# Reordered steps in the attention half and an earlier first gather, in a fused attention and mixture-of-experts kernel

## The reference

```python
xn = layernorm(x)                           # x: 8 x 512 tokens, 256 channels, float32
out = x + attention(xn) + experts(xn)

# attention: 16 heads of 16 features, causal
A = tril(1 + s + s*s/2)                     # s = q.k/4, a Taylor series in place of exp
y = (A @ v) / (row sums of A);  attention = y @ Wo.T

# experts: 8, the best 2 for each token, their weights a softmax over the two logits
y_e = (silu(xn @ W1[e]) * (xn @ W2[e])) @ W3[e]     # 256 -> 512 -> 256
```

## Time and profile before

| | |
|---|---|
| time, median of 3 runs | 669.97 us (669.42 to 671.02) |
| profiled execution | 669.97 us, span 668.2 us |
| TensorE busy | 96% of the span |
| VectorE, ScalarE, GpSimd busy | 61%, 51%, 51% |
| mean granted TensorE clock | 0.984 |

### The profile page before, as it was taken

The page is one execution under the profiler, slowest core; times in us unless marked ns, Lnnn a source line. Parts: engine busy times, 40 slices in busy tenths (PEclk is TensorE's granted clock), DMA queues, the critical chain, the costliest instruction groups (busy, mean ns, idle before and its releaser), DMA issues.

```text
span 668.2 us, 16297 instructions
## 1 busy us (share of the span) xinstructions
PE 640.6 (96%) x5351; PEld 493.3 (74%) x5351; DVE 409.9 (61%) x1067; ACT 341.9 (51%) x515; POOL 344.1 (51%) x381
## 2 busy tenths in 40 slices
PE   8799999999999999888999999999999999999994
PEld 6465666666666666546888888888888888888883
DVE  6776878787878585785984445444444544444452
ACT  3577878787877686764653223232322323232231
POOL 3255555546463736463464555555555545455542
PEclk9799999999999999987999999999999999999998
DMA  4643555455434435447533333334342333333332
GB/s 133 143 121 105 123 158 129 151 128 162 81 109 107 124 89 159 113 143 274 179 59 59 51 65 50 61 55 66 51 66 50 57 58 52 64 52 64 52 49 24
DMA packets 37773, 64.05 MB, mean 96 GB/s; under 512 B 8288, under 2 KB 25824, under 8 KB 37696
## 3 DMA queue, kind: packets, MB, share of 16 engines
q0 software_dynamic: 16704, 28.12, 21.4%
q1 hardware_dynamic: 20432, 34.24, 20.1%
q10 hardware_dynamic: 560, 0.66, 0.3%
HBM read 27.72 MB, written 22.68 MB: 75 GB/s over the span
## 4 chain that ended last, share of the span: by engine, by line
PE 87%; DVE 6%; ACT 2%; DMA 2%; issue 2%; ACTq 0%; POOL 0%; POOLq 0%; DVEq 0%
PE banks L1173 30%; PE banks L1194 15%; PE banks L1053 10%; PE banks L1035 8%; PE banks L1073 7%; PE banks L1182 5%; PE banks L1082 4%; PE banks L1117 4%; PE banks L1162 2%; PE banks L1102 1%; ACT T L530 1%; PE banks L1108 1%; DVE xTl L737 1%; PE banks L1091 1%; DMA out<-yo,xw 1%
## 5 line engine op out<-in xcount | busy, mean ns | idle before, releaser
L493 POOL DMA_INDIRECT out<-yo,xw x71 | 112.2, 1581 | 155.7 <-DVE yo L993 102.3
L622 ACT ACTIVATE sTh<-banks 128x512 fp32r<-128x512 f32 x71 | 42.5, 598 | 192.3 <-PE banks L1182 192.3
L473 POOL TENSOR_SCALAR_AFFINE_SELECT T<-T 128x512 f32<-128x512 f32 x128 | 80.6, 641 | 109.9 <-ACT T L536 41.7
L985 DVE TENSOR_TENSOR sTl<-banks,sTh 128x512 fp32r<-128x512 f32 x71 | 49.0, 691 | 118.0 <-ACT sTh L622 118.0
L1173 PE MATMUL banks<-w12h,xgh 128*128 x284 | 118.5, 417 | 0.9 <-DVE xgl L976 0.9
L1173 PE MATMUL banks<-w12l,xgh 128*128 x284 | 112.8, 397 | 0.0
L1173 PE MATMUL banks<-w12h,xgl 128*128 x284 | 112.6, 396 | 0.0
L482 POOL DMA_INDIRECT xg<-xs_scr,glist x71 | 73.4, 1033 | 21.5 <-issue 19.0
L1053 PE MATMUL banks<-T,vau 128*17 128x512 f32 (+3 forms) x1024 | 77.2, 441 | 0.2 <-POOL T L473 0.2
L1035 PE MATMUL banks<-Q,K 32*128 32x256 f32 (+2 forms) x1024 | 71.2, 363 | 6.0 <-DMA K<-Kt 2.8
L464 POOL DMA_INDIRECT xs_scr<-xb,slots x64 | 63.5, 993 | 18.8 <-issue 10.0
(11 more groups left out here) (172 smaller groups left out, 1212.6 us busy)
## 6 DMA issues: line engine op xcount, KB each, us to landing
Q<-Q SPq DMA_DIRECT2D x128, 64.0 KB, 2.3
w12r<-w SPq DMA_DIRECT2D x16, 512.0 KB, 4.8
out<-xa SPq DMA_DIRECT2D x16, 256.0 KB, 2.5
w3r<-w SPq DMA_DIRECT2D x8, 512.0 KB, 7.1
K<-Kt SPq DMA_DIRECT2D x124, 32.0 KB
xa<-x SPq DMA_DIRECT2D x7, 512.0 KB, 4.7
xg<-xs_scr,glist POOLq DMA_INDIRECT x71, 2.9
out<-yo,xw POOLq DMA_INDIRECT x71, 3.8
```

The source lines that it names most:

```text
L473: e.affine_select(out=v, in_=v, pattern=[[0, 4], [1, P]], compare_op=ALU.is_ge, fill=-1.0, base=0, channel_multiplier=-1).then_inc(s["g_mk ...
L493: e.indirect_dma_start(out, bass.IndirectOffsetOnAxis(xw[:, t % 4, NE:NE + 1].bitcast(U32), 0), yo[:, t % 2, :], None, compute_op=ALU.add) ...
L985: e.tensor_tensor(sTl[:], banks[:, 5, :], sTh[:].bitcast(F32), ALU.subtract).then_inc(s["v_st"], 1)
```

## The change

- The next batch's first K half is made first (quarter 1) and its Q half second (quarter 2), at the start too; `move_k` comes before `move_q` for it.
- VectorE takes the steps of `slot_b` as TensorE does: in quarters 0 and 2 step c comes before `normalise`.
- `place_rows` runs before `slot_b` in quarter 1 (so before `xTl`), `rsqrt` a little earlier, `w12_low` of quarter 2 after `slot_b`.
- Each send of batches 0 to 6 comes one slot earlier.
- In batch 7 the list work comes later relative to `o` and `normalise`; step G goes to `slot_c` of the last quarter.
- GpSimd issues the first gather between the second and third mask of the last quarter, after waits for the list and the sent rows.
- SyncE's w3 loads start in part one quarter earlier and are spread over later waits.
- TensorE's wait for all misc banks stands before the loop, so before `up(1, 0)`.

```diff
@@ slot_b, slot_c, sends_after
     elif qd == 2:
-        steps = [("c", b + 1, 1)]
+        steps = [("c", b + 1, 0)]
-    return steps + ([("t", ...)] if n else []) + ([("G", 0, 0)] if n == NQ - 1 else [])
+    return steps + ([("t", ...)] if n else [])
     if b == LAST:
-        return [("y", b, 0)] if qd == 3 else []
+        return [("G", 0, 0), ("y", b, 0)] if qd == 3 else []
-    return ([("c", b + 1, 0)] if qd == 1 else []) + [("v", ...), ("v", ...)]
+    return ([("c", b + 1, 1)] if qd == 1 else []) + [("v", ...), ("v", ...)]
-    k = 3 * qd + min(m, 2)
-    if k == 0:
-        return (b - 1, 7, 8) if b else None
-    i = k - (3 if b == LAST else 5)
+    i = 3 * qd + min(m, 2) - (3 if b == LAST else 4)
-FIRST = (("x", 0, 0), ("x", 0, 1), ("c", 0, 0), ("c", 0, 1), ...)
+FIRST = (("x", 0, 0), ("x", 0, 1), ("c", 0, 1), ("c", 0, 0), ...)
@@ sync_program
                     for h in range(2):
+                        move_k(e, b + 1, 0, h)
+                    for h in range(2):
                         move_q(e, b + 1, 0, h)
-                    for h in range(2):
-                        move_k(e, b + 1, 0, h)
@@
+            e.wait_ge(s["p_av"], NQ - 1)
             e.wait_ge(s["d_g1"], 16)
+            load_w3(0)
+            load_w3(1)
+            load_w12(13)
             e.wait_ge(s["p_av"], NQ)
-            for n in range(4):
-                load_w3(n)
-            load_w12(13)
-            e.wait_ge(s["p_t"], NQ)
-            for n in range(4, 6):
-                load_w3(n)
+            load_w3(2)
             store_out(LAST, 0)
             store_out(LAST, 1)
+            load_w3(3)
+            e.wait_ge(s["a_th"], 2)
+            load_w3(4)
+            e.wait_ge(s["p_t"], NQ)
+            load_w3(5)
+            e.wait_ge(s["a_th"], 3)
             done(e, "G", 0, 0)
             e.wait_ge(s["v_te"], 1)
-            for n in range(6, 8):
-                load_w3(n)
+            load_w3(6)
             e.wait_ge(s["p_o"], 2 * NBATCH)
             load_w12(14)
+            e.wait_ge(s["a_th"], 4)
+            load_w3(7)
@@ gpsimd_program, in mask(n)
                     if sends_after(n, m):
                         send(*sends_after(n, m))
+                    if n == NQ - 1 and m == 1:
+                        done(e, "G", 0, 0)
+                        e.wait_ge(s["d_xs0"], 512)
+                        e.wait_ge(s["d_xs1"], 512)
+                        e.wait_ge(s["d_z"], 32)
+                        e.wait_ge(s["p_s"], 6 * NQ - 8)
+                        gather(0)
@@ vector_program, before_b
-                elif n == NQ - 3:
+                elif n == NQ - 2:
+                    tile_gaps()
+                elif n == NQ - 1:
+                    all_rows()
+                elif qd == 1 and b < LAST:
+                    places(b)
+                    place_rows(b)
+                elif qd == 2 and b < NBATCH - 2:
+                    variance(b + 2)
+                elif qd == 3 and b < LAST:
+                    top(b + 1, 1)
@@ after_b (n == NQ - 3: tiles, NQ - 2: tile_rows(0), NQ - 1: expert_ends)
-                elif qd == 1 and b < LAST:
-                    place_rows(b)
-                if n == NQ - 2:
-                    w12_low(8)
+                if qd == 2 and (b, qd) in W12_LOW_WITH:
+                    w12_low(W12_LOW_WITH[b, qd])
@@ after_c (n == NQ - 3: tile_starts, NQ - 2: tile_rows(1), NQ - 1: experts)
                 elif qd == 2 and b < LAST:
                     top(b + 1, 0)
+                    if b < NBATCH - 2:
+                        rsqrt(b + 2)
@@ the loop of vector_program
-                items = slot_b(n)
-                if n % 4 in (0, 2) and n // 4 < LAST:
-                    items = [i for i in items if i[0] != "c"] + [i for i in items if i[0] == "c"]
-                for item in items:
+                for item in slot_b(n):
                     step(*item)
@@ tensor_program
+            for m in range(3):
+                e.wait_ge(s[f"m{m}"], USED[m])
             for t in range(1, NT + 1):
                 if t < NT:
                     expert_of(t)
                     up(t, 0)
-                if t == 1:
-                    for m in range(3):
-                        e.wait_ge(s[f"m{m}"], USED[m])
                 transpose_s(t - 1)
```

More of the change, by code:

```diff
@@ L27 @@
 W12_WITH = {(1, 1): 0, (1, 2): 1, (2, 1): 2, (2, 2): 3, (3, 1): 4, (3, 2): 5, (4, 1): 6, (4, 2): 7, (7, 0): 8}
-W12_LOW_WITH = {(1, 2): 0, (1, 3): 1, (2, 2): 2, (2, 3): 3, (3, 2): 4, (3, 3): 5, (4, 2): 6, (4, 3): 7}
+W12_LOW_WITH = {(1, 2): 0, (1, 3): 1, (2, 2): 2, (2, 3): 3, (3, 2): 4, (3, 3): 5, (4, 2): 6, (4, 3): 7, (7, 2): 8}
 F32 = mybir.dt.float32
@@ L56, in slot_b @@
     elif qd == 2:
-        steps = [("c", b + 1, 1)]
+        steps = [("c", b + 1, 0)]
     else:
         steps = [("o", b - 1, 0)] if b else []
-    return steps + ([("t", (n - 1) // 4, (n - 1) % 4)] if n else []) + ([("G", 0, 0)] if n == NQ - 1 else [])
+    return steps + ([("t", (n - 1) // 4, (n - 1) % 4)] if n else [])
 def slot_c(n):
@@ L68, in slot_c @@
     if b == LAST:
-        return [("y", b, 0)] if qd == 3 else []
+        return [("G", 0, 0), ("y", b, 0)] if qd == 3 else []
     if qd == 3:
         return ([("o", b - 1, 1)] if b else []) + [("y", b, 0), ("C", b + 1, 0)]
-    return ([("c", b + 1, 0)] if qd == 1 else []) + [("v", b + 1, 2 * qd - 2), ("v", b + 1, 2 * qd - 1)]
+    return ([("c", b + 1, 1)] if qd == 1 else []) + [("v", b + 1, 2 * qd - 2), ("v", b + 1, 2 * qd - 1)]
 def sends_after(n, m):
@@ L86, in sends_after @@
     return (b, i, i + 1) if 0 <= i < 8 else None
-FIRST = (("x", 0, 0), ("x", 0, 1), ("c", 0, 0), ("c", 0, 1), *(("v", 0, i) for i in range(4)))
+FIRST = (("x", 0, 0), ("x", 0, 1), ("c", 0, 1), ("c", 0, 0), *(("v", 0, i) for i in range(4)))
 END = (("t", LAST, 3), ("y", LAST, 1), ("o", LAST, 0), ("o", LAST, 1))
 def made(b, k):
-    return 4 * b + k + 1
+    return 4 * b + (2 - k if k < 2 else k + 1)
 def misc_uses():
@@ L498, in gpsimd_program @@
                 mask(n)
-            done(e, "G", 0, 0)
             e.wait_ge(s["p_s"], 6 * NQ)
[L501 to L504, removed]
+            for t in range(1, GR):
                 gather(t)
@@ L900, in before_b, with after_b @@
                     gates(b)
-                elif n == NQ - 3:
+                elif n == NQ - 2:
[9 more added lines that the diff above has]
+                    top(b + 1, 1)
+            def after_b(n):
+                b, qd = divmod(n, 4)
+                if n == NQ - 3:
                     tiles()
@@ L904, in before_b @@
                     tile_rows(0)
-                elif qd == 1 and b < LAST:
-                    places(b)
-                elif qd == 2:
-                    if b < NBATCH - 2:
-                        variance(b + 2)
-                    if (b, qd) in W12_LOW_WITH:
-                        w12_low(W12_LOW_WITH[b, qd])
-                elif qd == 3 and b < LAST:
-                    top(b + 1, 1)
-                    if b < NBATCH - 2:
-                        rsqrt(b + 2)
-            def after_b(n):
-                b, qd = divmod(n, 4)
-                if n == NQ - 3:
-                    tile_starts()
-                elif n == NQ - 2:
-                    tile_rows(1)
                 elif n == NQ - 1:
@@ L947, in after_c @@
                 elif n == NQ - 3:
-                    tile_gaps()
+                    tile_starts()
                 elif n == NQ - 2:
-                    all_rows()
+                    tile_rows(1)
                 elif n == NQ - 1:
```

## The result

The changed kernel takes 688.25 us (median of three; 687.91 to 689.13) against 669.97: a ratio of 1.026 (95% interval 1.024 to 1.029), 18.3 us slower. I forecast 680.2 us and a range of 673 to 687. The direction was right, the size too small by 8 us. Its profiled execution took 690.13 us, a span of 688.4, the longest of its six executions (spans 684.8 to 688.4). So the next pages ask where some 18 us are, and treat the last 2 of this one trace apart.

A forecast was written before the change was run, and what follows sets the result against it. TensorE, busy 640.6 of 668.2 us, was taken as the bound, so only its short waits counted. Terms 0.3 + 3.6 + 4.2 + 2.2 - 0.1 = 10.2 us on 669.97 gave 680.2 us, range 673 to 687.

The forecast's parts named there:

- Quarter 0: Batches 1 to 6: Q half ahead of normalise makes TensorE's step y wait for normalise; 6 x 0.6 = 3.6 us slower.
- quarter 1: place_rows before xTl, stretched by GpSimd's select, makes xTl 0.6 us late for TensorE; 7 x 0.6 = 4.2 us (1.4 to 5.0).
- V's fourth block: Quarters 1 and 2: the block's bank is freed by the later Q half, not Kt; 0.3 us x 7 = 2.2 us.
- Start: At the kernel's start, K half first makes the Q half and its moves later, delaying scores; +0.3 us (-0.7 to +1.4).
- The wait of `Kt`: VectorE stands some 2 us before Kt for the last K moves; copy_yw still reaches TensorE's transposes in time; counted nothing.
- Rival 2: Moves land 1 us later than counted, so copy_yw misses the transposes in some batches; +2.8 us, 683 us; chance 0.10.
- Moving rsqrt and the unit conversion: In the batches, both fill VectorE's idle time ahead of later copies: nothing; without that cover 0.6 and 1.2 us a batch.
- the hand-over "-0.1": Batch 7 to FFN: masks end later, gathered rows come sooner; first FFN matmul at 305.4 against 305.51, -0.1 us (-0.5 to +0.9).
- the misc banks' wait: Before the second FFN tile TensorE stands 0.8 us for VectorE's release, regained at later waits; taken as 0, bound 0.8.
- Rival 4: Faster by the hand-over: earlier gather 0 shrinks TensorE's idle and avoids the half clock; -4.5 us, 665.5 us; chance 0.07.
- rival 1: Granted clock falls inside batches after TensorE's longer xTl wait, in four of seven batches; +6.8 us, 687 us; chance 0.13.
- "Nothing shows": Rival 3: the 0.6, 0.6 and 0.3 us overlap other TensorE waits; within 1.3 us of 670; chance 0.08.

The follow-up runs named there:

- The two experiments: The changed kernel with the unit conversion back ahead of the Q half in quarter 2, 683.11 us; and with Q first, K second again, 681.35 us.
- the two tries from before: Kernel before with normalise ahead of the Q half in batch 7's quarter 0 too, 667.64 us; the same plus quarter 1's transposes behind the following scores, 672.20 us.
- the fastest kernel: Kernel before with one line changed: step c ahead of normalise in quarter 2 only, so normalise first in batch 7's quarter 0 too; 667.64 us, 0.9970.

## Why the prediction was right, and where it failed

*Quarter 0, quarter 1, V's fourth block.* All three held in mechanism and place, and within 0.1 us each time. Setting back the first and the second showed them one by one. For the second the choice of 0.6 near the upper end was right: VectorE's multiply, begun at 184.30 beside GpSimd's select of 184.22 to 184.85, was done only at 184.90, 0.60 us against 0.19. The Trainium skill's rule (SBUF — State Buffer, "SBUF: two separate sides") agrees with that row.

*Start.* The scores began at 20.55 us, 0.8 later than before, and the first attend 0.4 later. The 0.62 us for a move is that of Q's (four in 2.49 us in before); the earlier trace rows, named for it, has K's, at 0.79. The rest of the sum comes out of its rows.

*The wait of `Kt`.* It held in batches 1 to 6: VectorE stood, TensorE didn't. In batch 0, where only the 0.6 us of quarter 1 covered it, it did not. VectorE, then TensorE of after in batch 0:
```profile
42.99 0.69 DVE L755 TENSOR_TENSOR Kt<-banks,K 128x512 fp32r<-128x512 f32 x1 [4.44 <-DMA K<-Kt]
```
```profile
46.54 0.63 PE L1101 MATMUL banks<-ident,yw 128*128 128x128 f32 x4 [1.16 <-DVE yw L722]
```
The prediction had named the thinner cover and still counted nothing; that was 1.1 us. Rival 2 is this mechanism, once rather than in some batches.

*The step that failed: "Moving rsqrt and the unit conversion fills VectorE's idle time ahead of later copies: nothing. Without that cover, 0.6 us and 1.2 us a batch."* In the new order there is no idle time there. I had read VectorE's idle before copy_yw in the kernel before (0.99 us at 189.15) and not asked how the other edits move that stretch. K-first makes the Q half, 1.23 us and not 0.69, the last of the two, late because of ScalarE; behind it the conversion falls under two of GpSimd's selects and takes 2.18 us rather than 1.22. Rows of exactly that kind were in the prediction for place_rows; I applied them to the small operation and not to the large one. It cost 3.7 us, nearly half of what was missing. The two experiments show the cause from both sides, and the batches of one trace part the stretching from the place: with normalise set back the conversion stood in its new place in every batch, and quarters 2 and 3 took 0.9 us more than with it in its old place (17.37) where it was held, and 0.2 to 0.5 where it came first and the selects were held. So 0.5 to 0.7 us of the 0.92 hang on which of the two engines begins first. That is luck: of the 24 moved conversions in the six traces that leave K first and normalise last, 19 took 2.2 us, and 5 got in between the two selects, took 1.6 to 1.7 and held the second. Quarter 3 was 9.84 to 9.87 us with the former and 9.38 to 9.48 with the latter.

*The second: the hand-over "-0.1".* Two of its numbers failed. I let gather 0 start when the list was there, near 299.5. In the time of before (15.8 us less) it started at 300.8, since the rows passed their wait only at 299.7 and 1.1 us more went by to its start. The first I had bounded from above but not taken, the second I had left out, though the gather of before shows only 0.15 us because it was long past its waits. So the masks ended at 303.1, not 301.8. Some 1.0 us of that is the instruction packet beside the last send, which no row of the prediction showed; where the packet came after the send, gather 0 started 8.6 us after the attend of quarter 30, which is 299.8 in the time of before, and the masks ended at 302.0, close to the forecast. TensorE still waited 1.3 us for them. And "of which the wait for the rows goes": it went (it was 0.73 us), but the first FFN matmul came 4.9 us after the masks, and not 3.6, because TensorE's clock, counted from the masks, fell sooner. Windows of after and of before at the same distance from the masks' end (columns as in the earlier trace rows, with all engines):
```profile
321.00:323.00 2.00, 1.32 (x8) 0.95 (x7) 1.28 (x5) 0.38 (x1) 1.17 (x2) 0.50 0.48 121
```
```profile
303.00:305.00 2.00, 1.20 (x8) 0.62 (x6) 1.03 (x4) 0.42 (x2) 1.39 (x3) 0.97 0.34 107
```
The granted clock is 0.50 (1.2 GHz) where it was 0.97; it comes back sooner too, which gives about 1 us of the 2.5 back by the fourth tile. It fell at 320.67 and, before, at 304.86, both 13.7 us after the attend of quarter 30, so the 2.10 us of idle for the masks are not shown to be its cause. With the misc banks' wait (taken as 0, bound 0.8, measured 0.7) the whole is 2.05 us. That is the difference of two single traces, and the same way (32.40 and 34.45 us) follows how long the clock is 0.50 on it. It is so for some 10 us in both. With 3.4 us of it the way is 30.44 and 30.48 us in the two tries from before, which have the old hand-over, and 31.41 to 32.78 in four kernels with the new: 0.9 to 2.3 us. Rival 4 fell: with the hand-over alone the kernel is slower than before.

*The rivals.* In after the clock did not fall in the batches, for all of TensorE's idle of 1.18 us. The window of after over batches 0 to 6 and most of 7, granted clock in the third column from the end:
```profile
30.00:305.00 275.00, 254.00 (x2922) 163.09 (x2922) 197.52 (x605) 202.25 (x259) 145.11 (x195) 1.00 0.48 121
```
In four of the other traces (the conversion, K first or the w3 loads set back; the last sends earlier) it did fall once inside batch 7, about 9 us ahead of the attend of quarter 30, behind the first of that batch's two idle stretches of 0.99 us and not the second. The way between two attends was 9.6 us there in place of 7.91. So what rival 1 describes does happen, but at a place that had the same idle before the change. "Nothing shows" fell with the first line of the waits.

*The sum of the parts.* The seven kernels with one part set back gain 0.7, 0.6, 0.8, 0.9, 0.4, 0.3 and 0.0 percent, 3.7 in all, against 2.6 for the whole. Of the difference of 1.1 points, 7 us, setting the conversion back and setting K-first back account for some 3 us, as both take away the wait of quarter 3. Setting normalise back took part of it away too, 1.9 us in its trace. The rest is no more than the spread of seven medians allows.

*Open.* Why single executions have FFN tiles of 5.0 to 6.1 us: the load order is excluded, the cause is not known. It makes up some 2 us of the profiled execution. The other part of the spread within one kernel that the traces show is the clock: around the hand-over it was 0.50 for 3.4 us in some and for up to 13.7 us in others, and why it falls in one place or the other is open. That also bears on the 2.0 us of the fastest kernel: its trace has 3.4 us of half clock there, that of before some 10, and at the attend of quarter 30, before most of that, it is 1.0 us ahead.

## What to carry to other kernels

Price a set of moves together: lay out the new order of the engine that they share, with the operations behind the wait, before calling any of them covered; a hole seen in the old trace may be closed by the next edit. An operation moved into an idle stretch takes the duration that its new neighbours give it, so look at what the other engines run there and at which begins first; where that is a matter of 0.1 us, give the cost as a range. And a wait on TensorE is only gained by filling it with work that stood behind it; work that stood ahead moves the wait along.

## What the runs showed of the hardware

Of a VectorE operation with two inputs in SBUF and GpSimd's selects beside it, the one that began later was held. VectorE was held: 0.60 or 0.70 us in place of 0.19 for 128x32 beside a select of 0.63 to 0.65, done 0.05 us after it; 2.18 in place of 1.22 for 128x1024 beside two selects of 1.21 (197.25 to 198.46), done 1.1 us after them. GpSimd was held: two selects took 2.25 us beside a conversion that began 0.04 us ahead of them, and 1.87 beside one that began 0.42 us ahead, in place of 1.21. GpSimd's indirect send that followed right behind a conversion of 2.18 us took 1.81 us where it normally takes 0.98.

Rows sent to the scratch in HBM by an indirect DMA let GpSimd pass its wait for them 2.5 us after the issue in six traces with the new hand-over and 3.6 to 3.8 us in three; in the three a packet of 16 KB of the instruction queue (1.19 us in after) ran beside them, and one of the sixteen updates was late. From the last wait passed to the start of the gather behind it GpSimd needed 1.1 us, which vanishes where the wait has been passed during other work (0.15 us of idle in before).

The granted clock did not do the same each time at one place. Two idle stretches of 0.99 us stand 8 to 10 us apart in batch 7 of eleven traces, before and after among them; it fell to 0.50 within 2 us behind the first in four, behind the second in four, and behind neither in three.
